# Layer 0's first half: biases accumulated by TensorE and x1 taken out by ScalarE, in a four-layer residual kernel

## What is computed

```python
x = x + _L0_cond_ref(x, itok_B_0_7, L0_cond_weights, fside_8xS_0)   # w[idx] over positions, plus bias[idx]
x = x + _L1_cond_ref(x, Wg, Wu, Wd, Ag, Bg, Au, Bu, Ad, Bd, itok_B_0_7)   # gated MLP 512-2048-512 with adapters
x = x + _L2_cond_ref(x, W, A, Bm, scalings, itok_B_0_6)   # linear 512-512 with adapters
x = x + _L3_cond_ref(x, itok_B_1_198, weights)   # w[idx] over positions
```

## Time and profile before

| | |
|---|---|
| device time, median of 3 runs | 747.61 us (747.02 to 748.23) |
| device time of the profiled execution | 747.92 us |
| its span in the trace | 746.1 us |
| TensorE busy, share of the span | 718.5 us, 96% |
| weight loads | 609.3 us, 82% |
| VectorE | 584.3 us, 78% |
| ScalarE | 286.1 us, 38% |
| GpSimd | 269.6 us, 36% |
| granted TensorE clock, mean | 0.995 |

### The profile page before, as it was taken

One profiled execution on the slowest core, in us unless ns is written; L12 is line 12 of the kernel. 1 busy time (PEld: TensorE's weight loads), 2 busy tenths in 40 slices (PEclk: granted clock), 3 DMA queues, 4 the chain that ended last, 5 costly groups with the idle time before them and its releaser, 6 DMA issues.

```text
span 746.1 us, 10624 instructions
## 1 busy us (share of the span) xinstructions
PE 718.5 (96%) x3666; PEld 609.3 (82%) x3666; DVE 584.3 (78%) x979; ACT 286.1 (38%) x502; POOL 269.6 (36%) x489
## 2 busy tenths in 40 slices
PE   8689999999999999989899999999999999999997
PEld 8577788888888888868678888888888888788885
DVE  8968877888787878699798979787878786864542
ACT  3443423343434334244343333342424332334444
POOL 5936423242424241450338252534354231312100
PEclk9999999999999999999999999999999999999999
DMA  8485512121212221404623222221222043211112
GB/s 227 97 145 160 151 57 86 57 85 58 86 56 85 58 91 61 83 23 142 225 85 102 78 86 78 70 85 61 85 64 86 29 139 89 84 29 62 53 57 84
DMA packets 80725, 66.02 MB, mean 88 GB/s; under 512 B 42912, under 2 KB 65440, under 8 KB 80672
## 3 DMA queue, kind: packets, MB, share of 16 engines
q1 hardware_dynamic: 73056, 45.92, 21.0%
q0 software_dynamic: 7296, 19.41, 8.6%
q10 hardware_dynamic: 320, 0.02, 0.0%
HBM read 56.94 MB, written 8.39 MB: 88 GB/s over the span
## 4 chain that ended last, share of the span: by engine, by line
PE 83%; DVE 9%; issue 5%; ACT 1%; DMA 1%; POOL 0%; POOLq 0%; DVEq 0%; ACTq 0%
PE bank L1411 36%; PE bank L1532 21%; PE bank L1419 7%; PE bank L1663 5%; PE bank L1542 4%; PE bank L1652 2%; PE bank L1680 2%; PE bank L1639 1%; PE bank L1669 1%; DVE XC L921 1%; PE bank L1364 1%; PE bank L1352 1%; DVE hid L1045 1%; DMA BR<-in_L_cond_Bu_dram,boffs 1%; PE bank L1388 1%
## 5 line engine op out<-in xcount | busy, mean ns | idle before, releaser
L1411 PE MATMUL bank<-XC,WC 128*128 128x512 f32 x1344 | 333.2, 394 | 11.7 <-DVE XC L921 4.5
L1411 PEld LDWEIGHTS bank<-XC,WC 128*128 128x128 f32 x1344 | 244.6, 189 | 60.3 <-issue 6.9
L1532 PE MATMUL bank<-hs,wds 128*128 128x512 f32 x768 | 187.6, 394 | 5.2 <-DVE wds L1004 4.1
L1532 PEld LDWEIGHTS bank<-hs,wds 128*128 128x128 f32 x768 | 142.8, 190 | 34.3 <-DVE wds L1004 4.6
L421 POOL DMA_INDIRECT BR<-in_L_cond_Bu_dram,boffs x64 | 74.3, 1161 | 250.1 <-DVE BL L998 235.5
L421 POOL DMA_INDIRECT BR<-in_L_cond_Bg_dram,boffs x64 | 75.7, 1184 | 88.8 <-DVE BL L998 73.1
L641 ACT ACTIVATE hs<-hid 128x512 fp32r<-128x512 f32 x64 | 40.3, 630 | 166.0 <-DVE hid L1045 110.7
L1062 DVE TENSOR_TENSOR XA<-bank,XA 128x512 f32<-128x512 f32 x128 | 86.6, 686 | 16.4 <-PE bank L1532 14.3
L635 ACT ACTIVATE hid<-hid 128x512 f32<-128x512 f32 x48 | 30.3, 633 | 151.7 <-DVE hid L1028 81.2
L1419 PEld LDWEIGHTS bank<-UT,BL 128*128 128x128 f32 x512 | 76.5, 190 | 10.2 <-issue 1.5
L1419 PE MATMUL bank<-UT,BL 128*128 128x256 f32 x512 | 81.9, 283 | 1.2 <-DVE hid L1042 0.9
(11 more groups left out here) (164 smaller groups left out, 806.7 us busy)
## 6 DMA issues: line engine op xcount, KB each, us to landing
RW<-in_L_cond_Wg_dram SPq DMA_DIRECT2D x16, 512.0 KB, 3.4
RW<-in_L_cond_Wu_dram SPq DMA_DIRECT2D x16, 512.0 KB, 3.5
RD<-in_L_cond_Wd_dram SPq DMA_DIRECT2D x16, 512.0 KB, 3.5
out_dram<-XB SPq DMA_DIRECT2D x16, 256.0 KB, 2.2
XB<-in_x_dram SPq DMA_DIRECT2D x8, 256.0 KB, 6.1
x1park<-XB SPq DMA_DIRECT2D x8, 256.0 KB, 4.6
x2park<-XA SPq DMA_DIRECT2D x8, 256.0 KB, 2.5
XA<-x1park SPq DMA_DIRECT2D x4, 512.0 KB, 6.9
```

The source lines that it names most:

```text
L1411: last = nc.tensor.matmul(psum[:, :], WC[:, t, left, a, k, :], XC[:, right, b, k, :], start=(first and k == 0 and n == 0), stop=(k == 1 an ...
L1532: last = nc.tensor.matmul(psD[j % 2][:, :], by_feature(wds[:, f, a, :])[:, j % KT, :], hs[:, f, b, j // KT * 512:(j // KT + 1) * 512], sta ...
```

## The change

In layer 0 all 16 pairs now get their biases from a fifth matmul on TensorE; `biases_to_all`, `bias_copies` and the table `bias_all` go. The warm-up is one run of 30 matmuls. The first half's x1 is taken out by ScalarE's `xr_copy`, as the second half's was, and VectorE's `xr_sum` goes. ScalarE's and VectorE's lists are put in another order. SyncE's wait for `s_xr` ahead of the loads of `ad_raw` goes, as that buffer no longer holds the biases.

```diff
--- before.py
+++ after.py
@@ -109,7 +109,6 @@
         xin = [udp[:, s * FEAT:(s + 1) * FEAT] for s in range(2)] + [RD[:, s, :] for s in range(2)]
 
         bsel = wds[:, :, :, :].rearrange("p f a o -> p (f a o)")[0:BROWS, :]
-        bias_all = ad_raw[:, 0:HP, :].rearrange("p f m -> p (f m)")
         bias_high = BL[32:BROWS, 0, 0, 0:POS]
         xfirst = XB[:, :, :].rearrange("p k t -> p (k t)").rearrange("p (a t) -> p a t", t=FEAT)
 
@@ -216,8 +215,7 @@
         s_xin = [sem(f"s_xin{s}") for s in range(XIN)]
         s_x1st = sem("s_x1st")
         s_w0 = sem("s_w0")
-        s_w0c, s_braw, s_bias, s_bones, s_ball, s_l0, s_xr = (sem(n) for n in
-            ("s_w0c", "s_braw", "s_bias", "s_bones", "s_ball", "s_l0", "s_xr"))
+        s_w0c, s_braw, s_bias, s_l0, s_xr = (sem(n) for n in ("s_w0c", "s_braw", "s_bias", "s_l0", "s_xr"))
         s_xt = [sem(f"s_xt{k}") for k in range(4)]
         s_xch, s_xcl = sem("s_xch"), sem("s_xcl")
         s_al, s_araw, s_asum, s_auh, s_aul, s_u, s_sel = (sem(n) for n in
@@ -328,8 +326,6 @@
                 load_idx(2, idx_c)
                 load_u(0)
                 load_g(1)
-
-                sp.wait_ge(s_xr, HP)
                 for n in range(ADAPTERS):
                     sp.dma_start(ad_raw[:, :, n * RANK:(n + 1) * RANK],
                                  ad[n].rearrange("(k p) r -> p k r", p=P)).then_inc(s_ald, 16)
@@ -527,11 +523,6 @@
                 for row in (0, 32):
                     act.dma_start(biasraw[row:row + ADAPTERS, :], bias0).then_inc(s_small, 16)
 
-                def bias_copies():
-                    for t in range(2):
-                        act.wait_ge(s_bones, t + 1)
-                        nc.scalar.activation(bias_all[:, t * 512:(t + 1) * 512], (psB, psC)[t][:, :], ACT.Copy).then_inc(s_ball, 1)
-
                 def xr_copy(p):
 
                     act.wait_ge(s_l0, p + 1)
@@ -684,13 +675,19 @@
 
                 act.wait_ge(s_ones, 1)
                 nc.scalar.activation(early[:, :], ones[:, 0:1].bitcast(f32), ACT.Silu)
-                bias_copies()
                 act.dma_start(idx[:, 1, :], idx_b.partition_broadcast(P)).then_inc(s_idx[1], 16)
                 act.dma_start(scal[:, :], scal2.partition_broadcast(P)).then_inc(s_scal, 16)
+                for p in range(3):
+                    xr_copy(p)
                 raw_high(G, 0, None, s_gld)
+                xr_copy(3)
                 xc_high(0, B11)
+                xr_copy(4)
                 xc_high(0, B21)
+                xr_copy(5)
                 sums_high(G, 0)
+                xr_copy(6)
+                xr_copy(7)
                 xc_high(0, B22)
                 xc_high(0, T3)
                 xr_copy(HP)
@@ -908,14 +905,6 @@
                     link(nc.vector.tensor_scalar(mask2[:, :], idxf[:, 1, :], row_f[:, 1:2], srow[:, 0:1],
                                                  ALU.is_equal, ALU.mult))
 
-                def xr_sum(p):
-                    if p % 4 == 0:
-                        dve.wait_ge(s_ball, p // 4 + 1)
-                    dve.wait_ge(s_l0, p + 1)
-                    at = p * P
-                    nc.vector.tensor_tensor(XA[:, :, at:at + P], l0_bank(p)[:, :].rearrange("p (k t) -> p k t", k=KT),
-                                            bias_all[:, at:at + P].unsqueeze(1).to_broadcast([P, KT, P]), ALU.add).then_inc(s_xr, 1)
-
                 def xc_low(h, slot):
                     dve.wait_ge(s_xch, filled(h, slot))
                     nc.vector.tensor_tensor(XC[:, slot, 1, :, :], xc_raw[h][slot], XC[:, slot, 0, :, :].bitcast(f32),
@@ -1180,23 +1169,16 @@
                 layer3_zeros()
                 biases(1)
                 move_matrices()
-                for p in range(3):
-                    xr_sum(p)
                 g_combine(0)
-                xr_sum(3)
                 raw_low(G, 0)
-                xr_sum(4)
-                xr_sum(5)
                 masks()
                 xc_low(0, B11)
-                xr_sum(6)
-                xr_sum(7)
+                xc_low(0, B21)
+                sums_low(G, 0)
                 t3_sum(0)
-                xc_low(0, B21)
                 t2_sum(0)
                 xc_low(0, B22)
                 xc_low(0, T3)
-                sums_low(G, 0)
                 t1_sum(0)
                 xc_low(0, T2)
                 a_low(0, 0)
@@ -1361,13 +1343,10 @@
                     if p >= 3:
                         pe.wait_ge(s_xr, p - 2)
                     for k in range(KT):
-                        last = nc.tensor.matmul(l0_bank(p)[:, k * P:(k + 1) * P], by_feature(x_of(p))[:, k, :], w0bd_of(p),
-                                                start=(k == 0), stop=(p < HP and k == KT - 1), skip_group_check=True)
-                    if p < HP:
-                        last.then_inc(s_l0, 1)
-                        return
-                    if p == HP:
-                        pe.wait_ge(s_bias, 2)
+                        nc.tensor.matmul(l0_bank(p)[:, k * P:(k + 1) * P], by_feature(x_of(p))[:, k, :], w0bd_of(p),
+                                                start=(k == 0), stop=False, skip_group_check=True)
+                    if p % HP == 0:
+                        pe.wait_ge(s_bias, p // HP + 1)
                     nc.tensor.matmul(l0_bank(p)[:, :].rearrange("p (k t) -> p k t", k=KT), ones[0:BROWS, :],
                                      bsel[:, p * P:(p + 1) * P].unsqueeze(1).to_broadcast([BROWS, KT, P]),
                                      start=False, stop=True, skip_group_check=True).then_inc(s_l0, 1)
@@ -1589,15 +1568,7 @@
                         downs(unit - 1, at)
                     c12_product(n, U)
 
-                def biases_to_all():
-                    pe.wait_ge(s_bias, 1)
-                    for t in range(2):
-                        nc.tensor.matmul((psB, psC)[t][:, :], ones[0:BROWS, :], bsel[:, t * 512:(t + 1) * 512],
-                                         start=True, stop=True).then_inc(s_bones, 1)
-
-                warm(24)
-                biases_to_all()
-                warm(4)
+                warm(30)
                 for p in range(HP):
                     layer0(p)
                 layer0(HP)
```

## The result

The kernel after takes **758.07 us** (756.76 to 758.45, four runs), the kernel before 747.38 (747.02 to 748.23, four runs) on the same chip: ratio 1.013, interval 1.012 to 1.015. The forecast was 745.8, 744.8 to 747.7. It is wrong in sign. The profiled execution of after has 756.76 us with a span of 754.9, against 747.92 and 746.1 before.

The account below looks back on a forecast made before the run. TensorE's start of line 1388 was taken to bound the kernel: 34.49 to 32.45 us gains 2.04, plus 0.1 for its slow first records, 2.1 in all. 747.92 - 2.1 = 745.8 us, range 744.8 to 747.7.

Parts of the forecast that it names:

- The step that failed: TensorE, layer 0's first pairs: full clock taken from 10.8 us as in the kernel before, pair 1 ending at 11.8.
- Each further pair takes 1.51: TensorE, layer 0 after pair 1: 1.51 us per pair, pair 7 ending at 20.9, pair 9 at 23.9.
- Pair 0 takes 8 x 0.21: TensorE, first pair of layer 0: eight records at six a us, then its bias matmul, ending at 9.85.
- 0.6 for the bias: TensorE, first pair of layer 0: 0.6 us for the added bias matmul.
- T3 must wait for pair 7: 21.6: VectorE: its instruction T3 waits for TensorE's pair 7 and starts at 21.6 us, against 21.82 before.
- to 29.0: VectorE: six instructions instead of eight from T3 to T2's low part, 7.4 us, ending at 29.0 instead of 31.65.
- Line 1388 starts at 32.45, and not at 30.5: First adapter product on TensorE: GpSimd's copies, held up by VectorE, let it start at 32.45 us, against 34.49 before.
- the rival of 750.3: GpSimd gets nothing past until VectorE stops; line 1388 starts at 36.9, 2.4 us later, 750.3 in all; chance 0.05.
- The first rival: TensorE's clock falls in front of line 1388, costing 1.2 to 1.7 us: 747.0 to 747.5; chance 0.38.

Follow-up runs that it names:

- experiment 10: The change with the first half's bias matmuls reading all 128 rows (zero-padded by GpSimd) in place of 40; 748.37 us, ratio 1.001.
- Experiment 2: The changed kernel with ScalarE's loads of `idx` and `scal` put behind its first copy of x1; 754.09 us.
- experiment 3: The changed kernel with 15 plain fp32 warm-up matmuls in place of 30 fp32r ones; 747.62 us.
- experiment 4: The changed kernel with both the loads of `idx` and `scal` late and the 15 plain fp32 warm-up matmuls; median 747.13 us, ratio 0.999.
- experiment 7: Experiment 4's kernel with VectorE's two-input instructions of 1,024 columns in the first half each split in two; median 745.29 us, ratio 0.998.
- experiment 11: Experiment 4's kernel with eight fp32 filler matmuls ahead of P6 and eight behind it; 744.95 us, ratio 0.996.
- experiment 6: The kernel before with its warm-up (24 and 4 matmuls) made of 12 and 2 in plain fp32; median 746.75 us, ratio 0.999.
- experiment 1: The kernel before with an unread 40-row, 512-column bias matmul added behind each of layer 0's first eight pairs; 759.09 us.
- experiment 5: Experiment 4's kernel with eight fp32 filler matmuls added between P6 and the first adapter product; median 745.41 us, ratio 0.997.
- experiment 12: Experiment 11's kernel with four fillers behind P6 and GpSimd's 16 adapter copies ahead of its placements for pairs 12 and 13; 744.29 us, ratio 0.995.

## Why the prediction was wrong, step by step

**The step that failed** is one clause under TensorE: "From 10.8 on the records of line 1364 came twice as fast [...]; I take the same moment: pair 1 ends at 11.8." It took the rise of the clock as a date. It is a consequence of what TensorE runs. With the 40-row matmuls between the pairs the clock stayed at 1.2 GHz up to 41.6, so the pairs took 2.73 us instead of the 1.51 of the sum, and P1 came at 36.39 instead of 23.9. None of my rivals had a clock that does not rise; the one on the clock was about a fall of 3.4 us. What rows of before could have told: the rise came while TensorE was at 48 records (24 matmuls) of 128 rows with nothing between them, and the change takes exactly that away. Price, by the medians of experiment 10: some 9.5 us. Why 40 rows do this stays open.

**A term left out.** I priced the removal of `bias_copies` on ScalarE and not the two loads queued behind it, which moved 5.5 us forward, in among the first tiles. Experiment 2 prices it: pair 0 comes 1.6 us earlier, the span is 2.6 shorter (the clock, which rose 3.9 earlier there, at 37.65, gives the rest). With the clock up it is less: from experiment 3 to 4 pair 0 comes 0.9 earlier, P5 1.2.

**TensorE's pairs.** "Each further pair takes 1.51" is right at 2.4 GHz (experiment 4: 14.93 to 16.44). "Pair 0 takes 8 x 0.21" was 8 x 0.25, 1.98 us (9.14 to 11.12): the "six records a us" of the earlier trace rows count every record that touches the microsecond. Its "0.6 for the bias" was 0.7.

**VectorE.** "T3 must wait for pair 7: 21.6", "to 29.0": in experiment 4 T3 began at 20.8 and the low part of T2 ended at 28.5. Right, once the clock is up.

**GpSimd.** "Line 1388 starts at 32.45, and not at 30.5": 32.73 in experiment 4, with the copies from 29.26. Right, and experiment 7 confirms the reason. The rows decided rightly between two readings of the rule. The Trainium skill (SBUF — State Buffer, "SBUF: two separate sides") has the other engine blocked fully while the first holds the ports, and that for its whole instruction. Experiment 4 agrees as far as single instructions go: of the 12 placements in 12.48 us, nine meet VectorE's run of nine long instructions, and one gets past per instruction, 1.27 us apart (experiment 7 doubled the instructions, and 1.7 times as much got past). What is refuted is the strict reading, that nothing gets past a run without gaps, and with it the rival of 750.3.

**The first rival** (chance 0.38) is what experiments 3 and 4 show: a fall in line 1388 (at 34.24 and 35.09), 747.1 to 747.6. Its place was right, and its price nearly: from line 1388 to P5 both take 7.41 us, against 5.89 with the clock up (experiment 11), 1.5 more, within the rival's 1.2 to 1.7.

**Reading before's own time.** Between 356.67 and 384.37 us before's profiled execution has a wait of 0.88 us for VectorE's `hid` (at 376.6), and the stretch takes 27.7 us. In ten of the thirteen other traces the same piece of TensorE's list takes 26.5 to 26.6, experiment 6, the kernel before with another warm-up, among them; in experiments 1, 10 and 4 it takes 26.7, 26.8 and 27.1. (So the change is 10.0 us late at 357 and 8.8 at 393.) That difference of up to 1.2 us belongs to the execution, or to how the units happen to fall, and not to the change; why it varies I have not settled. A sum against one profiled execution inherits this, and so do the small gains above: against before, P5 moved by -1.1, +0.5 and -0.1 us in experiments 5, 6 and 7, the medians by -2.0, -0.6 and -2.1. What lies between is not explained by the start.

## What to carry to other kernels

Before matmuls are added between others, compare the rows they fill: a few short matmuls with 40 of 128 rows on a TensorE that has not reached 2.4 GHz can hold it at 1.2. Padding them to 128 rows with zeros cost TensorE nothing here (0.77 for 0.79 us each at 1.2 GHz, 0.48 for 0.50 at 2.4), but writing the zeros delayed pair 0 by 1.1 us. When a step is taken off an engine's list, every DMA behind it on that list moves forward, so ask what it will meet there. A gain that opens pauses on TensorE, here of 1.6 and 2.5 us, can be given back in the clock; fillers that kept the engine at work in both secured the gain here (P5 at 38.60 for 40.14).

## What the runs showed of the hardware that was not expected

- **Rows and the clock.** Same place, nearly the same length (0.79 and 0.77 us), same kind: with 40 rows the clock stayed at 1.2 GHz to 48.5 us, with 128 it rose at 12.1. Once up, 40-row matmuls between the pairs did not bring it down (experiments 3, 4, 5, 7, 11 and 12, 9 to 28 us).
- **Rows and the pace.** A pair with its bias matmul takes 1.12 us with 128 rows (16.07 to 17.19, experiment 10) and 1.51 with 40 (experiment 4), both at 2.4 GHz. The smaller matmul costs 0.4 us more. I did not try what makes it so.
- **The kind of the warm-up.** Thirty fp32r matmuls of 128 columns, 6.7 us without a gap, did not raise the clock; fifteen in plain fp32, put in their place, had it up at 4.4 to 7.3 us in six traces. The Trainium skill (TensorE: Matmul & The Clock Gate, "Part 1: The HAM clock gate") lets sustained busy time bring the clock up, and makes no difference there by the rows or the type of the matmuls; the trace of after differs: TensorE was busy from 9.14 to 41.6 us without a gap in its timeline, and the clock stayed at 1.2 GHz.
- **Falls after short pauses.** After 1.6 us (experiment 5) the clock fell, at 29.97, in P6; after the same pause in experiment 4 only behind a second one of 2.5. The two kernels are the same up to there, so one execution differs from the next in this, and in when the clock rises (6.1 and 6.9 us). It was low for 3.4 or 6.8 us each time.
